# Four corners of the array for a chunk's value and output weight products: odd batches with the two heads exchanged

## Chip, cores and metric

One core of one Trainium2 chip. The metric is the device time of one execution in microseconds (us). Lower is better.

## What is computed

One pre-norm decoder layer on x of 4 x 512 rows and 256 columns: an attention across the rows of a group, a cross attention to a context of 4 batches of 64 rows, and a mixture of 8 experts. The change is in the cross attention (16 heads of 64, context `c`):

```python
q = (queries @ Wq + bq).reshape(bs, nq, H, D_KEY).transpose(0, 2, 1, 3)
k = (keys @ Wk + bk).reshape(bs, nk, H, D_KEY).transpose(0, 2, 1, 3)
v = (values @ Wv + bv).reshape(bs, nk, H, D_VALUE).transpose(0, 2, 1, 3)
att = jnp.einsum('bhqd,bhkd->bhqk', q, k) / np.sqrt(D_KEY).astype(np.float32)
att = jax.nn.softmax(att, axis=-1)
out = jnp.einsum('bhqk,bhkd->bhqd', att, v)
out = out.transpose(0, 2, 1, 3).reshape(bs, nq, H * D_VALUE)
return out @ Wo + bo
```

## The kernel before

The program is written engine by engine, each with its own instruction stream and with semaphores between them; the order of the work is the order in which the functions call their steps. There are four parts. Part 1 is the row attention and, between its steps, the preparation of the cross attention. Part 2 is the cross attention in 16 steps, one for each tile of 128 rows. Parts 3 and 4 are the routing and the experts.

The cross attention is folded into two tables that depend on the batch only. `G` is the query weight times the keys (line 765, `G_product`), so that the scores are the normalised rows times `G`. `H` is the values times the output weight (line 878, `pe_H`), so that the result is the transposed probabilities times `H`. Both are kept as two parts, `_hi` (rounded, copied by ScalarE: line 496 for G, line 889 for H) and `_lo` (the remainder, by VectorE: line 580 and line 897), and each later product is three matmuls (lines 917 to 919).

The 16 heads are handled in 8 chunks of two. For a chunk `c`, `V_T[:, c, b]` holds the values of batch `b`, head `2c` in partitions 0 to 63 and head `2c + 1` in 64 to 127; `Wo[:, c]` holds the matching rows of the output weight. Head 0's product of a batch is a 64x64 block of weights in the first 64 rows and first 64 columns of the array and gives partitions 0 to 63 of a bank, head 1's is in the other rows and columns and gives partitions 64 to 127. Two of the 4 batches stand side by side in one PSUM bank, and a chunk fills two banks, m = 0 and m = 1:

```python
for m in range(2):
    ps = bank_free(f"H{c}{m}")
    for b in (2 * m, 2 * m + 1):
        for rows in (slice(0, DK), slice(DK, P)):
            mm = t.matmul(ps[rows, (b % 2) * D:(b % 2 + 1) * D], V_T[rows, c, b], Wo[rows, c], ...)
    filled(mm, f"H{c}{m}")
```

`bank_free` makes TensorE wait until the bank's last user has been read, `filled` tells the readers. The banks of a chunk come from a table: `H_BANKS = ((4, 7), (5, 0), (1, 4), (7, 5), (4, 5), (7, 4), (5, 7), (4, 5))`. A bank is free when `H_lo` of its last user is made, as that is the second of its two readers.

The 8 chunks run in front of the first four steps of part 2 (`run_steps`, two chunks a step), mixed with the lead-in of the pipeline. TensorE's order is: chunks 0 and 1; transposes of the normalised rows of tile 0 (line 945); chunks 2 and 3; transposes of tile 1, scores of tile 0; chunks 4 and 5; transposes of tile 2, scores of tile 1; chunks 6 and 7; then the probability transposes of tile 0 (line 938), after which the 16 steps follow one another. After the scores, VectorE takes a maximum (`mx`, line 1160), subtracts it (`prob`, line 1165), and ScalarE takes the exponential (line 1026). On VectorE the chunks' `H_lo` stand in the same order as on TensorE, between `xT_lo` (line 1152), `mx`, `prob` and the sums of the exponentials (line 1138). On ScalarE chunk 5 stands behind the first exponential and the normalised rows of tile 2 (line 1200), chunk 7 behind the second and tile 3; `H_BEFORE_ACT` and `H_BEFORE_EXP` say so.

In part 1 the query weight is transposed into `WqT` (copied out of PSUM by VectorE, line 591; the bias's column by ScalarE, line 521). The scores' factor of `DK ** -0.5` is applied where G is copied. `of_head` gives the columns of G that belong to a head.

Of the kernel before, what the change touches and what calls it, by code (L numbers as in the profile page):

```python
# [13 lines left out]
def build_program(nc, A, out):  # L14
# [8 lines left out]
    ACT = mybir.ActivationFunctionType  # L23
    AX = mybir.AxisListType

    P = 128
    T, B, D = A["x"].shape
# [3 lines left out]
    MC = D // P  # L31
    HS = A["L0_attn_q_weight"].shape[1]
    HD = D // HS
    CB, CK, _ = A["ctx_1024"].shape
    HX = 16
    DK = A["L0_xattn_Wq"].shape[1] // HX
    HK = HX * CK
    NC = HX * DK // P
# [81 lines left out]
    with ctx:  # L120
# [6 lines left out]
        def overlay(*sets):  # L127
# [83 lines left out]
        bank = lambda i: ctx.enter_context(nc.psum_tensor(f"bank{i}", [P, 512], F32))  # L211
# [20 lines left out]
        WqT_ready, bq_placed, kv_ready = (  # L232
            sem(n) for n in ("WqT_ready", "bq_placed", "kv_ready"))
        G_hi_ready, G_ready = (sem(n) for n in ("G_hi_ready", "G_ready"))
        V_ready = sem("V_ready")
        H_hi_ready, H_ready = sem("H_hi_ready"), sem("H_ready")
# [52 lines left out]
        def bank_free(what):  # L289

            b, _, before = where[what]
            if before:
                nc.tensor.wait_ge(*before)
            return banks[b]

        def bank_full(eng, what):

            b, n, _ = where[what]
            eng.wait_ge(full[b], n + 1)
            return banks[b]  # L300

        def filled(mm, what):
            mm.then_inc(full[where[what][0]], 1)

        block = ctx.enter_context(nc.Block())
        v3 = lambda ap, a: ap.rearrange("p (a n) -> p a n", a=a)
        raw = lambda ap: ap.bitcast(F32)
        by_chunk = lambda bank: v3(bank[:], MC * CB)

        def of_head(G, c, h):  # L310

            return G[:].rearrange("p m b n -> p (m b) n")[:, :, c * P + h * DK:c * P + (h + 1) * DK]

# [114 lines left out]
        def act_part1(act):  # L430
            a = nc.scalar
# [60 lines left out]
            def G_evac(c):  # L492

                for h in range(2):
                    ps = bank_full(act, f"G{c}{h}")
                    a.activation(of_head(G_hi, c, h), by_chunk(ps), ACT.Copy, scale=DK ** -0.5).then_inc(G_hi_ready, 1)

            act.wait_ge(ident_ready, 1)
            a.activation(warm[:], ident[:, 0:1], ACT.Exp)
# [10 lines left out]
            ps = bank_full(act, "ctxT")  # L510
# [5 lines left out]
            ps = bank_full(act, "owT")  # L516
# [1 line left out]
            squares(0)  # L518
            xnT_evac(1)
            ps = bank_full(act, "cols")  # L520
            a.activation(WqT[:, :, D - 1], ps[:, 0:NC], ACT.Copy).then_inc(bq_placed, 1)
            a.activation(bias_cols[:], ps[:, 0:3 * NC], ACT.Copy).then_inc(cols_ready, 1)
            a.activation(b1_cols[:], ps[:, 32:32 + E * FC], ACT.Copy).then_inc(cols_ready, 1)

# [5 lines left out]
            ps = bank_full(act, "N")  # L530
# [6 lines left out]
            xnT_evac(3)  # L537
            q_evac(2)
            G_evac(0)
            mixT_evac(0)  # L540
            squares(2)
            KV_evac(1)
            G_evac(1)
            weights_of(2)
            q_evac(3)
            mixT_evac(1)
            squares(3)
            KV_evac(2)
            G_evac(2)
            weights_of(3)  # L550
            KV_evac(3)
# [12 lines left out]
        def dve_part1(dve, order):  # L564
            v = nc.vector
# [9 lines left out]
            def low_parts(c):  # L575

                for h in range(2):
                    ps = bank_full(dve, f"G{c}{h}")
                    dve.wait_ge(G_hi_ready, 2 * c + h + 1)
                    v.scalar_tensor_tensor(out=of_head(G_lo, c, h), in0=by_chunk(ps), scalar=DK ** -0.5,  # L580
                                           in1=raw(of_head(G_hi, c, h)), op0=ALU.mult,
                                           op1=ALU.subtract).then_inc(G_ready, 1)

            def WqT_evac(k):

                ps = v3(bank_full(dve, f"WqT{k}")[:], 2)
                for c in range(2):  # L590
                    ins = v.tensor_scalar(WqT[:, 2 * k + c, 0:D - 1], ps[:, c, 0:D - 1], ps[:, c, D - 1:D], None,
                                          ALU.subtract)
                ins.then_inc(WqT_ready, 1)

            def add_residual(j):
# [56 lines left out]
            for j in range(1, NJ):  # L652
# [4 lines left out]
            ps = bank_full(dve, "MT")  # L657
            v.tensor_tensor(MTs[:], v3(ps[:, 0:MC * P], MC), mask16[:].unsqueeze(1).to_broadcast([P, MC, P]),
                            ALU.mult).then_inc(MT_ready, 1)
            distances(0)  # L660
            WqT_evac(0)
            weigh(0)
            differences(1)
            WqT_evac(1)
            WqT_evac(2)
            distances(1)
            scale(0)
            WqT_evac(3)
            weigh(1)
            differences(2)  # L670
            low_parts(0)
            distances(2)
            scale(1)
            add_residual(0)
            weigh(2)
            differences(3)
            low_parts(1)
            distances(3)
            scale(2)
            add_residual(1)  # L680
            weigh(3)
            low_parts(2)
            statistics2(0)
            dve.wait_ge(consts_ready, 1)
# [181 lines left out]
        def pe_H(pe):  # L866

            t = nc.tensor

            def H_chunk(c):  # L870
                if c == 0:
                    pe.wait_ge(xn3_stored, 16)
                pe.wait_ge(V_ready, c + 1)
                for m in range(2):
                    ps = bank_free(f"H{c}{m}")
                    for b in (2 * m, 2 * m + 1):
                        for rows in (slice(0, DK), slice(DK, P)):
                            mm = t.matmul(ps[rows, (b % 2) * D:(b % 2 + 1) * D], V_T[rows, c, b], Wo[rows, c],
                                          start=True, stop=True)
                    filled(mm, f"H{c}{m}")  # L880
            return H_chunk

        def act_H(act):
            a = nc.scalar

            def H_chunk(c):
                for m in range(2):
                    ps = bank_full(act, f"H{c}{m}")
                    a.activation(H_hi[:, 2 * m:2 * m + 2, c], v3(ps[:], 2), ACT.Copy).then_inc(H_hi_ready, 1)
            return H_chunk  # L890

        def dve_H(dve):
            def H_chunk(c):
                for m in range(2):
                    ps = bank_full(dve, f"H{c}{m}")
                    dve.wait_ge(H_hi_ready, 2 * c + m + 1)
                    nc.vector.tensor_tensor(H_lo[:, 2 * m:2 * m + 2, c], v3(ps[:], 2), raw(H_hi[:, 2 * m:2 * m + 2, c]),
                                            ALU.subtract).then_inc(H_ready, 1)
            return H_chunk

# [779 lines left out]
        @block.scalar  # L1680
        def _(act):
            act_part1(act)
            act_part2(act)
            act_part3(act)
            act_part4(act)
# [32 lines left out]
```

## Time and profile before

| | |
|---|---|
| runs | 373.85, 373.59, 373.82 us (median 373.82) |
| span of the profiled execution | 370.1 us |
| instructions in it | 6439 |
| TensorE matmul busy | 319.9 us (86%) |
| VectorE busy | 287.2 us (78%) |
| ScalarE busy | 184.1 us (50%) |
| GpSimd busy | 195.2 us (53%) |

The span runs from the first to the last instruction of one profiled execution; the runs' times have in them what lies before and after it as well. Which of the three runs is nearest to the profiled one isn't told. Matmuls are pipelined, so that a busy TensorE is not one at its peak, and one fp32 matmul of the program shows as two records. All times of the rows below are in us from the start of the span. PE is TensorE (PEld its weight loads), DVE VectorE, ACT ScalarE, POOL GpSimd.

### The profile page before, as it was taken

What the parts mean: (1) busy time and instruction counts of PE and PEld (TensorE: products, weight loads), DVE (VectorE), ACT (ScalarE), POOL (GpSimd) and SP (SyncE); (2) the same over time, 40 slices, a digit from 0 to 9 for tenths busy, and PEclk for the clock granted to TensorE, in tenths of its full rate; (3) what the DMA queues carried; (4) which work ended last, traced back from release to release, by engine and by line L of the source; (5) the groups of instructions that cost most, each with busy time, mean ns of one, the idle gap of its engine ahead of it and who ended that gap; (6) DMA issues with size and microseconds to landing.
All of it is one profiled execution on the core that took longest, in us unless ns stands there. A gap on an engine that the chain in (4) does not pass through costs nothing.

```text
span 370.1 us, 6439 instructions
## 1 busy us (share of the span) xinstructions
PE 319.9 (86%) x2346; PEld 288.5 (78%) x2346; DVE 287.2 (78%) x659; ACT 184.1 (50%) x357; POOL 195.2 (53%) x247
## 2 busy tenths in 40 slices
PE   8889998899979999999999861116999999999991
PEld 7767886675569999999999851005999999999991
DVE  3898887948888988888888727787588699799850
ACT  2677554555545556775675432362317456652230
POOL 3787889713223468778878766003405515533222
PEclk9999999999999999999999985555999999999998
DMA  7950000000000306306215237001149657612222
GB/s 248 392 192 1 2 0 2 0 0 3 0 2 14 129 29 186 128 16 200 74 70 184 66 121 270 0 1 28 58 127 267 168 193 217 171 16 43 30 30 28
DMA packets 24047, 34.29 MB, mean 93 GB/s; under 512 B 1784, under 2 KB 20560, under 8 KB 23888
## 3 DMA queue, kind: packets, MB, share of 16 engines
q1 hardware_dynamic: 20112, 29.36, 23.7%
q0 software_dynamic: 3072, 4.20, 6.3%
q10 hardware_dynamic: 832, 0.32, 0.4%
q8 instruction: 19, 0.31, 0.3%
q14 instruction: 12, 0.10, 0.1%
HBM read 27.58 MB, written 6.29 MB: 92 GB/s over the span
## 4 chain that ended last, share of the span: by engine, by line
PE 69%; DVE 15%; POOL 7%; ACT 4%; issue 3%; DMA 1%; ACTq 0%; DVEq 0%; POOLq 0%
PE bank L917 12%; PE bank L919 12%; PE bank L918 12%; PE q_banks L917 4%; PE q_banks L918 4%; PE q_banks L919 4%; PE bank L938 4%; DVE flags_all L1271 3%; PE q_banks L718 2%; PE bank L1444 2%; PE bank L736 2%; PE bank L752 2%; PE bank L982 1%; POOL acc L410 1%; DMA X<-in_x 1%
## 5 line engine op out<-in xcount | busy, mean ns | idle before, releaser
L1569 POOL DMA_INDIRECT out_x<-ybuf,idx x16 | 26.3, 1641 | 59.8 <-DVE ybuf L1588 57.7
L1046 POOL TENSOR_TENSOR prob<-prob,rsum 128x1024 f32<-128x1024 f32 x16 | 30.5, 1905 | 18.8 <-DVE rsum L1144 17.3
L917 PE MATMUL bank<-H_hi,PT_hi 128*128 128x256 f32 x128 | 36.3, 284 | 1.7 <-DVE PT_lo L1115 1.7
L917 PE MATMUL bank<-W_hi,h_hi 128*128 128x256 f32 x128 | 37.2, 291 | 0.0
L919 PE MATMUL bank<-H_hi,PT_lo 128*128 128x256 f32 x128 | 36.2, 283 | 0.0
L918 PE MATMUL bank<-H_lo,PT_hi 128*128 128x256 f32 x128 | 36.2, 283 | 0.0
L919 PE MATMUL bank<-W_hi,h_lo 128*128 128x256 f32 x128 | 36.2, 283 | 0.0
L918 PE MATMUL bank<-W_lo,h_hi 128*128 128x256 f32 x128 | 36.2, 283 | 0.0
L1549 POOL DMA_INDIRECT xg<-xn_rows,idx x16 | 18.5, 1158 | 29.5 <-DVE idx L1615 25.3
L1026 ACT ACTIVATE prob<-prob 128x1024 f32<-128x1024 f32 x16 | 16.9, 1059 | 33.5 <-DVE prob L1165 33.4
L1526 ACT ACTIVATE hbuf<-bank,b_cols 128x256 f32<-128x256 f32 x32 | 13.4, 472 | 40.1 <-PE bank L919 40.1
L1099 POOL TENSOR_TENSOR W_lo<-W_raw,W_hi 128x1024 fp32r<-128x1024 f32 x12 | 28.6, 2386 | 0.0
L917 PEld LDWEIGHTS bank<-H_hi,PT_hi 128*128 128x128 f32 x128 | 24.5, 191 | 2.7 <-issue 2.1
L918 PEld LDWEIGHTS bank<-H_lo,PT_hi 128*128 128x128 f32 x128 | 24.5, 191 | 0.5
L917 PEld LDWEIGHTS bank<-W_hi,h_hi 128*128 128x128 f32 x128 | 24.7, 193 | 0.2 <-DVE h_lo L1649 0.2
L918 PEld LDWEIGHTS bank<-W_lo,h_hi 128*128 128x128 f32 x128 | 24.6, 192 | 0.0
L919 PEld LDWEIGHTS bank<-W_hi,h_lo 128*128 128x128 f32 x128 | 24.5, 192 | 0.0
L919 PEld LDWEIGHTS bank<-H_hi,PT_lo 128*128 128x128 f32 x128 | 24.5, 191 | 0.0
L1647 DVE CAST h_hi<-hbuf 128x512 fp32r<-128x512 f32 x32 | 13.8, 432 | 13.2 <-ACT hbuf L1526 13.1
L1649 DVE TENSOR_TENSOR h_lo<-hbuf,h_hi 128x512 fp32r<-128x512 f32 x32 | 22.2, 692 | 1.1
L1600 DVE TENSOR_TENSOR W_lo<-W_raw,W_hi 128x2048 fp32r<-128x2048 f32 x10 | 22.7, 2284 | 0.0
L1115 DVE TENSOR_TENSOR PT_lo<-bank,PT_hi 128x512 fp32r<-128x512 f32 x32 | 20.1, 669 | 0.6 <-ACT PT_hi L998 0.6
(269 smaller groups left out, 1063.6 us busy)
## 6 DMA issues: line engine op xcount, KB each, us to landing
W_raw<-in_L_ffn_W SPq DMA_DIRECT2D x16, 1024.0 KB, 5.7
X<-in_x SPq DMA_DIRECT2D x4, 512.0 KB, 6.2
xn_rows<-xn SPq DMA_DIRECT2D x16, 128.0 KB, 1.7
out_x<-X SPq DMA_DIRECT2D x4, 512.0 KB, 3.5
Wq<-in_L_xattn_Wq SPq DMA_DIRECT2D x1, 1024.0 KB, 10.9
Wk<-in_L_xattn_Wk SPq DMA_DIRECT2D x1, 1024.0 KB, 13.8
Wv<-in_L_xattn_Wv SPq DMA_DIRECT2D x1, 1024.0 KB, 15.0
Wo<-in_L_xattn_Wo SPq DMA_DIRECT2D x1, 1024.0 KB, 16.9
```

The costliest lines, as they stand in the source:

```text
L917: t.matmul(out_ps, hi, rhs_hi, start=first, stop=False)
L918: t.matmul(out_ps, hi, rhs_lo, start=False, stop=False)
L919: return t.matmul(out_ps, lo, rhs_hi, start=False, stop=last_one)
L938: mm = t.transpose(banks[4 + g][:, c * P:(c + 1) * P], flat[:, o:o + P], ident[:])
L1026: a.activation(prob[:, s], prob[:, s], ACT.Exp).then_inc(exp_ready, 1)
L1046: g.tensor_tensor(prob[:, s], prob[:, s], rsum[:, s].unsqueeze(2).to_broadcast([P, HX, CK]), ALU.mult).then_inc(prob_ready, 1)
L1099: nc.gpsimd.tensor_tensor(lo[at], W[at], raw(hi[at]), ALU.subtract).then_inc(ready, 1)
L1115: v.tensor_tensor(PT_lo[:, cur.slot, c], v3(banks[4 + g][:], 4), raw(PT_hi[:, cur.slot, c]), ALU.subtract).then_inc(PT_ready, 1)
L1549: g.indirect_dma_start(xg[:, s, h], None, xn3_dram, bass.IndirectOffsetOnAxis(ap=idx[:, e, h:h + 1], axis=0), bounds_check=last_row, oob_i ...
L1569: g.indirect_dma_start(out_flat, bass.IndirectOffsetOnAxis(ap=idx[:, e, h:h + 1], axis=0), ybuf[:, h], None, bounds_check=last_row, oob_is ...
L1600: v.tensor_tensor(lo[at], W[at], raw(hi[at]), ALU.subtract).then_inc(late, 1)
L1649: v.tensor_tensor(h_lo[:, fs], hbuf[:, g_ % 2], raw(h_hi[:, fs]), ALU.subtract).then_inc(h_ready, 1)
```

## The change

In an odd batch the two heads of a chunk change places in the output: head 0's product goes to partitions 64 to 127 of the bank, head 1's to 0 to 63. Batches 0 and 2 now share the chunk's first bank, 1 and 3 its second, so that the four products of an even and an odd batch use the four 64x64 corners of the array. Both banks are waited for ahead of the chunk's first product; the first is told full after batch 2, the second after batch 3. The copies of H write every other batch. So that the probabilities, whose order is that of G's columns, meet the same order in H, `of_head` exchanges the two heads' columns of G in the odd batches. That makes the pattern of its copies longer by one loop, and the factor `DK ** -0.5` moves from them into `WqT` and the bias's column; `G_lo` becomes a plain subtraction.

```diff
@@ -305,11 +305,14 @@
         block = ctx.enter_context(nc.Block())
         v3 = lambda ap, a: ap.rearrange("p (a n) -> p a n", a=a)
         raw = lambda ap: ap.bitcast(F32)
-        by_chunk = lambda bank: v3(bank[:], MC * CB)
+        by_chunk = lambda bank: bank[:].rearrange("p (a b n) -> p a b n", b=2, n=DK)
 
         def of_head(G, c, h):
 
-            return G[:].rearrange("p m b n -> p (m b) n")[:, :, c * P + h * DK:c * P + (h + 1) * DK]
+            first = G[:, 0, 0, c * P + h * DK:c * P + (h + 1) * DK]
+            across, along = first.ap
+            return bass.AP(first.tensor, first.offset,
+                           [across, [2 * HK, MC * CB // 2], [HK + (DK if h == 0 else -DK), 2], along])
 
 
 
@@ -493,7 +496,7 @@
 
                 for h in range(2):
                     ps = bank_full(act, f"G{c}{h}")
-                    a.activation(of_head(G_hi, c, h), by_chunk(ps), ACT.Copy, scale=DK ** -0.5).then_inc(G_hi_ready, 1)
+                    a.activation(of_head(G_hi, c, h), by_chunk(ps), ACT.Copy).then_inc(G_hi_ready, 1)
 
             act.wait_ge(ident_ready, 1)
             a.activation(warm[:], ident[:, 0:1], ACT.Exp)
@@ -518,7 +521,7 @@
             squares(0)
             xnT_evac(1)
             ps = bank_full(act, "cols")
-            a.activation(WqT[:, :, D - 1], ps[:, 0:NC], ACT.Copy).then_inc(bq_placed, 1)
+            a.activation(WqT[:, :, D - 1], ps[:, 0:NC], ACT.Copy, scale=DK ** -0.5).then_inc(bq_placed, 1)
             a.activation(bias_cols[:], ps[:, 0:3 * NC], ACT.Copy).then_inc(cols_ready, 1)
             a.activation(b1_cols[:], ps[:, 32:32 + E * FC], ACT.Copy).then_inc(cols_ready, 1)
 
@@ -577,9 +580,8 @@
                 for h in range(2):
                     ps = bank_full(dve, f"G{c}{h}")
                     dve.wait_ge(G_hi_ready, 2 * c + h + 1)
-                    v.scalar_tensor_tensor(out=of_head(G_lo, c, h), in0=by_chunk(ps), scalar=DK ** -0.5,
-                                           in1=raw(of_head(G_hi, c, h)), op0=ALU.mult,
-                                           op1=ALU.subtract).then_inc(G_ready, 1)
+                    v.tensor_tensor(of_head(G_lo, c, h), by_chunk(ps), raw(of_head(G_hi, c, h)),
+                                    ALU.subtract).then_inc(G_ready, 1)
 
             def WqT_evac(k):
 
@@ -588,8 +590,8 @@
 
                 ps = v3(bank_full(dve, f"WqT{k}")[:], 2)
                 for c in range(2):
-                    ins = v.tensor_scalar(WqT[:, 2 * k + c, 0:D - 1], ps[:, c, 0:D - 1], ps[:, c, D - 1:D], None,
-                                          ALU.subtract)
+                    ins = v.tensor_scalar(WqT[:, 2 * k + c, 0:D - 1], ps[:, c, 0:D - 1], ps[:, c, D - 1:D],
+                                          DK ** -0.5, ALU.subtract, ALU.mult)
                 ins.then_inc(WqT_ready, 1)
 
             def add_residual(j):
@@ -871,13 +873,14 @@
                 if c == 0:
                     pe.wait_ge(xn3_stored, 16)
                 pe.wait_ge(V_ready, c + 1)
-                for m in range(2):
-                    ps = bank_free(f"H{c}{m}")
-                    for b in (2 * m, 2 * m + 1):
-                        for rows in (slice(0, DK), slice(DK, P)):
-                            mm = t.matmul(ps[rows, (b % 2) * D:(b % 2 + 1) * D], V_T[rows, c, b], Wo[rows, c],
-                                          start=True, stop=True)
-                    filled(mm, f"H{c}{m}")
+                halves = (slice(0, DK), slice(DK, P))
+                ps = [bank_free(f"H{c}{m}") for m in range(2)]
+                for b in range(CB):
+                    for h in range(2):
+                        mm = t.matmul(ps[b % 2][halves[h ^ (b % 2)], (b // 2) * D:(b // 2 + 1) * D],
+                                      V_T[halves[h], c, b], Wo[halves[h], c], start=True, stop=True)
+                    if b >= 2:
+                        filled(mm, f"H{c}{b % 2}")
             return H_chunk
 
         def act_H(act):
@@ -886,7 +889,7 @@
             def H_chunk(c):
                 for m in range(2):
                     ps = bank_full(act, f"H{c}{m}")
-                    a.activation(H_hi[:, 2 * m:2 * m + 2, c], v3(ps[:], 2), ACT.Copy).then_inc(H_hi_ready, 1)
+                    a.activation(H_hi[:, m:CB:2, c], v3(ps[:], 2), ACT.Copy).then_inc(H_hi_ready, 1)
             return H_chunk
 
         def dve_H(dve):
@@ -894,7 +897,7 @@
                 for m in range(2):
                     ps = bank_full(dve, f"H{c}{m}")
                     dve.wait_ge(H_hi_ready, 2 * c + m + 1)
-                    nc.vector.tensor_tensor(H_lo[:, 2 * m:2 * m + 2, c], v3(ps[:], 2), raw(H_hi[:, 2 * m:2 * m + 2, c]),
+                    nc.vector.tensor_tensor(H_lo[:, m:CB:2, c], v3(ps[:], 2), raw(H_hi[:, m:CB:2, c]),
                                             ALU.subtract).then_inc(H_ready, 1)
             return H_chunk
 
```

The order of TensorE between the first and the second scores, with chunks 4 (banks 4 and 5) and 5 (banks 7 and 4); a row is a matmul of the program, `xk` that many of them, and the semaphores for which the first waits stand behind it. Before:

```order
L919 MATMUL bank1<-G_hi,xT_lo 128x512
L878 MATMUL bank4<-Wo,V_T 64x256 [waits H_ready,V_ready]
L878 MATMUL bank4<-Wo,V_T 64x256 x3
L878 MATMUL bank5<-Wo,V_T 64x256 [waits H_ready]
L878 MATMUL bank5<-Wo,V_T 64x256 x3
L878 MATMUL bank7<-Wo,V_T 64x256 [waits H_ready,V_ready]
L878 MATMUL bank7<-Wo,V_T 64x256 x3
L878 MATMUL bank4<-Wo,V_T 64x256 [waits H_ready]
L878 MATMUL bank4<-Wo,V_T 64x256 x3
L945 MATMUL bank6<-ident,xn2 128x128 [waits xT_ready,xn2_ready]
```

Of the change:

```order
L922 MATMUL bank1<-G_hi,xT_lo 128x512
L880 MATMUL bank4<-Wo,V_T 64x256 [waits H_ready,V_ready]
L880 MATMUL bank4<-Wo,V_T 64x256
L880 MATMUL bank5<-Wo,V_T 64x256 x2
L880 MATMUL bank4<-Wo,V_T 64x256 x2
L880 MATMUL bank5<-Wo,V_T 64x256 x2
L880 MATMUL bank7<-Wo,V_T 64x256 [waits H_ready,V_ready]
L880 MATMUL bank7<-Wo,V_T 64x256
L880 MATMUL bank4<-Wo,V_T 64x256 x2
L880 MATMUL bank7<-Wo,V_T 64x256 x2
L880 MATMUL bank4<-Wo,V_T 64x256 x2
L948 MATMUL bank6<-ident,xn2 128x128 [waits xT_ready,xn2_ready]
```

A chunk's two banks now take turns, and its second wait has gone to its front: the first product of chunk 5, in bank 7, stands behind the wait for bank 4, which chunk 4's `H_lo` frees.

The order of TensorE ahead of the first scores, with chunks 2 (banks 1 and 4) and 3 (banks 7 and 5). Before:

```order
L878 MATMUL bank1<-Wo,V_T 64x256 [waits x1_ready,V_ready]
L878 MATMUL bank1<-Wo,V_T 64x256 x3
L878 MATMUL bank4<-Wo,V_T 64x256 [waits H_ready]
L878 MATMUL bank4<-Wo,V_T 64x256 x3
L878 MATMUL bank7<-Wo,V_T 64x256 [waits H_ready,V_ready]
L878 MATMUL bank7<-Wo,V_T 64x256 x3
L878 MATMUL bank5<-Wo,V_T 64x256 [waits H_ready]
L878 MATMUL bank5<-Wo,V_T 64x256 x3
L945 MATMUL bank6<-ident,xn2 128x128 [waits xT_ready,xn2_ready]
L945 MATMUL bank6<-ident,xn2 128x128
L917 MATMUL bank0<-G_hi,xT_hi 128x512 [waits H_ready,xT_ready]
```

Of the change:

```order
L880 MATMUL bank1<-Wo,V_T 64x256 [waits H_ready,x1_ready,V_ready]
L880 MATMUL bank1<-Wo,V_T 64x256
L880 MATMUL bank4<-Wo,V_T 64x256 x2
L880 MATMUL bank1<-Wo,V_T 64x256 x2
L880 MATMUL bank4<-Wo,V_T 64x256 x2
L880 MATMUL bank7<-Wo,V_T 64x256 [waits H_ready,V_ready]
L880 MATMUL bank7<-Wo,V_T 64x256
L880 MATMUL bank5<-Wo,V_T 64x256 x2
L880 MATMUL bank7<-Wo,V_T 64x256 x2
L880 MATMUL bank5<-Wo,V_T 64x256 x2
L948 MATMUL bank6<-ident,xn2 128x128 [waits xT_ready,xn2_ready]
```

The matmuls are as many as before; chunk 3 waits for bank 5 ahead of its products in bank 7.

## Rows read from the trace of the kernel before

**Rows 1.** The page: its first line, and the engines' shares of the chain.

```profile
span 370.1 us, 6439 instructions
PE 69%; DVE 15%; POOL 7%; ACT 4%; issue 3%; DMA 1%; ACTq 0%; DVEq 0%; POOLq 0%
```

**Rows 2.** The chain that ended last, by time: start us, us, what (xrecords).

```profile
30.05 3.72 PE q_banks L718 x16
...
58.37 1.06 PE q_banks L765 x8
...
85.12 3.60 PE bank L878 x32
...
89.33 0.23 PE bank L918
...
91.89 1.29 DVE mx L1160 x2
...
95.95 0.49 ACT H_hi L889
...
104.07 0.70 DVE H_lo L897
```

**Rows 3.** TensorE in order of time, 78 to 107 us: start us, us, what [idle before].

```profile
85.05 3.67 PE L878 MATMUL bank<-Wo,V_T 64*64 64x256 f32 x32
88.65 0.44 PE L945 MATMUL bank<-ident,xn 128*128 128x128 f32 x2
88.85 0.48 PE L917 MATMUL bank<-G_hi,xT_hi 128*128 128x512 f32 x1
...
91.78 2.81 PE L878 MATMUL bank<-Wo,V_T 64*64 64x256 f32 x24
95.02 1.08 PE L878 MATMUL bank<-Wo,V_T 64*64 64x256 f32 x8 [0.44 <-DVE H_lo L897]
96.03 0.44 PE L945 MATMUL bank<-ident,xn 128*128 128x128 f32 x2
...
104.91 1.16 PE L938 MATMUL bank<-ident,prob 128*128 128x128 f32 x8 [1.27 <-DVE H_lo L897]
```

**Rows 4.** VectorE in order of time, 78 to 107 us.

```profile
84.32 2.47 DVE L897 TENSOR_TENSOR H_lo<-bank,H_hi 128x512 fp32r<-128x512 f32 x4
86.70 0.42 DVE L1152 TENSOR_TENSOR xT_lo<-bank,xT_hi 128x256 fp32r<-128x256 f32 x1
87.04 1.40 DVE L897 TENSOR_TENSOR H_lo<-bank,H_hi 128x512 fp32r<-128x512 f32 x2
...
94.29 1.28 DVE L897 TENSOR_TENSOR H_lo<-bank,H_hi 128x512 fp32r<-128x512 f32 x2
96.53 1.29 DVE L897 TENSOR_TENSOR H_lo<-bank,H_hi 128x512 fp32r<-128x512 f32 x2 [0.97 <-ACT H_hi L889]
```

**Rows 5.** ScalarE in order of time, 78 to 107 us.

```profile
92.91 0.60 ACT L889 ACTIVATE H_hi<-bank 128x512 fp32r<-128x512 f32 x1 [3.26 <-PE bank L878]
...
95.86 1.06 ACT L889 ACTIVATE H_hi<-bank 128x512 fp32r<-128x512 f32 x2
```

**Rows 6.** Groups of instructions, whole span: xcount | busy us, mean ns | idle before.

```profile
L897 DVE TENSOR_TENSOR H_lo<-bank,H_hi 128x512 fp32r<-128x512 f32 x16 | 10.4, 685 | 2.3 <-ACT H_hi L889 2.3
L889 ACT ACTIVATE H_hi<-bank 128x512 fp32r<-128x512 f32 x16 | 9.2, 596 | 8.0 <-PE bank L878 8.0
L580 DVE SCALAR_TENSOR_TENSOR G_lo<-bank,G_hi 128x512 fp32r<-128x512 f32 x10 | 6.4, 680 | 2.8 <-ACT G_hi L496 2.8
L496 ACT ACTIVATE G_hi<-bank 128x512 fp32r<-128x512 f32 x10 | 5.5, 602 | 8.6 <-PE bank L765 8.6
```

**Rows 7.** Lines 591 and 650: duration ns min/median/max, first and last start us.

```profile
L591 DVE TENSOR_SCALAR WqT<-bank x8: 476/478/482, 20.9 to 32.0; 128x255 f32<-128x255 f32 x8
L650 DVE TENSOR_SCALAR xn<-X,mv,rstd x3: 414/502/557, 8.0 to 8.8; 128x256 f32<-128x256 f32 x3
```

**Rows 8.** Line 878's records from 95.02 to 95.3 us, the first of chunk 5's second half.

```profile
L878 PE MATMUL bank<-Wo,V_T x4: 376/402/427, 95.0 to 95.3; 64*64 64x256 f32 x4
```

## The prediction

> **What bounds the kernel now.** I read the page first [rows 1]: the span is 370.1 us and the chain that ended last runs 69% over TensorE and 15% over VectorE. The median of the runs is 373.82 us, so about 3.7 us lie around the span; the sum below is made against the span and carried over to the median as it is. A change of under 0.2% (0.75 us) is what a measurement of this kernel can hardly tell from none.
>
> Then I looked at what the edit touches: the products of chunks 0 to 7 (line 878), between 80 and 105 us. Two things stand in the chain of waits there [rows 2]. Before the first scores the chain runs through 32 records of line 878, that is TensorE bounds. After the scores it leaves TensorE: VectorE (`mx` and more), ScalarE (up to `H_hi`), VectorE (`H_lo`), and it comes back to TensorE only with the probability transposes of line 938. So the same products lie on the path once, and beside it twice. From 104.9 us on the chain is TensorE, step after step, and whatever is won or lost by then is carried to the end.
>
> One matmul of line 878 shows as two records. How much of the array is in use is read from the chain [rows 2]: the full 128x128 products of line 718 go one after the other, 16 records in 3.72 us, 0.23 us a record; line 878 does 32 records in 3.60 us, so two run at a time (heads 0 and 1, each in its corner). Four at a time would halve that.
>
> **What it removes, step one: chunks 2 and 3.** Today both take 3.67 us from 85.05 us, two transposes follow at 88.65, and the first scores start at 88.85 [rows 3]. A half chunk of 8 records takes 1.08 us to its last result (the row at 95.02) and lets the next start after 3.60/4 = 0.90 us; at four at a time these are the figures of a whole chunk. Chunk 2 still starts at 85.05. Chunk 3 now waits for both its banks at once: the later one is freed by the third of the four `H_lo` that start at 84.32 and take 2.47 us, 0.60 us apart and 0.68 us long, so at 86.2 [rows 4]. It runs from 86.25 to about 87.2, the transposes to 87.45. Then the scores meet their next wait, the one for chunk 2's first `H_lo`: it starts at 87.04 behind `xT_lo` (86.70) on VectorE [rows 4] and would not start earlier, since VectorE works without a pause from 84.3 to there; its `H_hi` is ready by then (85.05 + 1.08 + 0.60 = 86.7). It ends at 87.72, so the scores start at 87.8 in place of 88.85: **1.05 us won**. What is late next is VectorE. `mx`, which follows the scores, starts 1.05 us earlier too, at 90.8 for 91.89 [rows 2], as the copies of chunk 3 that stand ahead of it come forward with their products.
>
> **What it adds, step two: chunks 5 and 7.** Today the first half of chunk 5 runs right after chunk 4 (the 24 records at 91.78), and only its second half, in bank 4, waits for chunk 4's `H_lo` [rows 3]. Both bank waits now stand ahead of the chunk's first product, so the whole of it waits. This `H_lo` starts at 94.29 and ends at 94.97 [rows 4], and TensorE goes on at 95.02. At four at a time the chunk ends when its second half ends today, 1.08 us later at 96.10, and the transposes at 96.03 and the next scores are not moved. But its first bank is then full only at 96.10, where today it has long been full: ScalarE copies 0.05 us behind a full bank (91.78 + 1.08 = 92.86 against 92.91 [rows 5]), so at 96.15 where today it comes at 95.86, after `prob` and `xn` [rows 5]. That is 0.3 us, and nothing hides it: VectorE waits for exactly this copy, 0.97 us today [rows 4], and after its two `H_lo` it goes straight on to sums, `xT_lo` and the next `mx`. **0.3 us lost.** Chunk 7 is the same pattern 7.5 us later (`H_lo` at 104.07 in [rows 2]); its `H_lo` is what the transposes of line 938 wait for, 1.27 us today [rows 3]. **Another 0.3 us lost.**
>
> **The small edits.** The copies of G keep their count and size. `G_lo` goes from a scalar_tensor_tensor of 680 ns to a tensor_tensor, which at 128x512 from the same kind of memory takes 685 ns (`H_lo`); ScalarE's copy with a scale takes 602 ns, without one 596 (`H_hi`) [rows 6]. The swapped column order is a third loop in the pattern over the same 512 elements; the contiguous `H_lo` and the strided `G_lo` rows agree within 5 ns, so I cost it at nothing. The scale moves into `WqT`, whose tensor_scalar gets a second operation: 478 ns today, and the nearest row with two operations, line 650, runs 414 to 557 ns [rows 6, 7]. Two of the eight lie on the chain, so this is -0.13 to +0.16 us; I take zero, since the medians of 478 and 502 ns are nearest to no difference. The copy of the query bias into `WqT` (128x8) changes only its scale.
>
> **The sum**: -1.05 + 0.3 + 0.3 = -0.45 us, a span of 369.65 and **373.4 us** against the median.
>
> The unknown in it is one price: two blocks that share a row half but not a column half. No row shows that pair. Two rows stand near it. Line 765 has blocks that share all columns but no rows, and does 8 records in 1.06 us, also two at a time [rows 2]; and the scores' products take in 512 columns [rows 3] every 0.23 us (line 918 in [rows 2]), so the stream into one row half carries twice what one record of line 878 asks for (256 columns in 0.23 us). Both speak for four at a time, which I take. Ends: four at a time without any loss, -0.45 us; in between, the second block of a row half comes one record behind the first and shows its weight load, which I read as the 0.05 us by which a first record (427 ns) is longer than the others (376 ns) [rows 8]. The first bank is then full 0.1 us later and the second some 0.35; ScalarE's second copy is 0.48 us behind its first anyway, so a chunk loses 0.1 us more and the sum is -0.25 us.
> The Trainium skill, TensorE: Matmul & The Clock Gate (Part 3: Packing small matmuls), reports 16 blocks of 32x32 at 10.6 times the speed; no run here shows it, and by it the sum would be the -0.45 us.
>
> **The rivals.**
> *Two at a time, as now (slower).* If blocks of one row half exclude each other, a chunk takes 8 steps as today, and the first step is worth nothing: chunks 2 and 3 end at 88.65 again. The second step then costs the whole half that can no longer run ahead: chunk 5 starts at 95.02, its first bank is full two steps of 0.225 us before the end, 1.08 + 0.90 - 0.45 = 1.53 us later, and ScalarE copies at 96.60 in place of 95.86: 0.74 us lost, and as much again at chunk 7. Together +1.5 us, **375.3 us**; with a weight load of 0.05 us shown at each of three changes of block, some 0.2 us more, 375.5. It decides as soon as a chunk alone takes more than about 1.6 us. For it speaks that no row shows such a pair; against it the two rows above. It is also the case in which the change does not do what it says.
> The Trainium skill has two rules that would give this case. TensorE: Matmul & The Clock Gate (Part 3) says a weight load overlaps a running matmul only if the row group differs. TensorEngine Tiling (Restrictions and Gotchas) says that different row tiles cannot use one PSUM bank at once. The trace disagrees with the second as far as it can be seen: heads 0 and 1 write one bank from two row halves, and do so two at a time [rows 2].
> *The losses do not show (faster).* If a first bank were full 0.79 us after the chunk's start (95.86 - 0.05 - 95.02), ScalarE would find it ready, and the whole 1.05 us stays: **372.8 us**. Against it: each block has four records in a row, and half a chunk with the same four takes 1.08 us today [rows 3].
> *Part of both.* Two streams into a row half slow each other to a chunk of about 1.4 us: the first step still wins nearly all of its 1.05 us, the chunks lose some 0.5 us each, and the time is about that of before.
>
> **How the numbers follow.** Four at a time, with or without the one record's lag, 0.63: 373.4 us, its own range 373.1 to 373.7. Partly, 0.07: 373.8. Two at a time, 0.20: 375.3. Faster than the sum, 0.10: 372.8 or below. The range takes in the rival that is slower and leaves out half of the faster one: 372.8 to 375.4. Faster by over 0.2% takes the last case and a little of the first, 0.13; slower the second rival and a little of the part case, 0.23; the rest, 0.64, is within 0.2%.
>
> **What would show it.** Right: the records of the product line stand in 16s of about 1.1 us; the first scores start about 1 us earlier, at 87.8; the pause of VectorE ahead of the `H_lo` of chunks 5 and 7 grows from 0.97 to about 1.3 us; and line 938 starts about 0.45 us earlier than 104.91. Wrong: a chunk that takes 1.8 us or more alone, or first scores that start at 88.8 still; or a `WqT`, `G_hi` or `G_lo` whose mean moves by more than 50 ns.

## The result and the profile after

The changed kernel takes 378.38 us (median of 4 runs, 376.88 to 379.17) against 373.70 (4 runs, 373.37 to 373.85) before: ratio 1.0137, 95% interval 1.0109 to 1.0165. In a second set, with the experiments below, it took 377.46 us (6 runs) against 373.63 (29 runs), ratio 1.0107 (1.0067 to 1.0148). The forecast was 373.4 us, from 372.8 to 375.4: the change is slower, and by more than the range allowed.

Where the time went in the two profiled executions, by four marks in TensorE's order:

| stretch | before, us | after, us | difference |
|---|---|---|---|
| start to chunk 0's first product | 80.27 | 82.69 | +2.42 |
| from there to the first probability transposes | 24.64 | 25.47 | +0.83 |
| from there to the second (one step) | 6.82 | 9.24 | +2.42 |
| from there to the end | 258.4 | 259.9 | +1.5 |

The four differences add up to 7.2 us, more than the 4.7 of the medians, since the two profiled executions are not alike: every execution here takes 1.7 to 1.9 us more than its span, so the one before, with its span of 370.1 us, took about 372, while the changed one is the longest of its four (379.17). The marks before that are not shown above:

```profile
80.27 3.67 PE L878 MATMUL bank<-Wo,V_T 64*64 64x256 f32 x32
84.71 0.41 PE L945 MATMUL bank<-ident,xn 128*128 128x128 f32 x2 [0.77 <-DVE G_lo L580]
...
111.73 1.03 PE L938 MATMUL bank<-ident,prob 128*128 128x128 f32 x8
```

TensorE of the changed kernel in order of time (start us, us, what [idle before]; line 878 is now 880, 945 is 948, 938 is 941):

```profile
82.69 1.96 PE L880 MATMUL bank<-Wo,V_T 64*64 64x256 f32 x32
87.12 0.41 PE L948 MATMUL bank<-ident,xn 128*128 128x128 f32 x2 [2.48 <-DVE G_lo L583]
87.55 2.29 PE L880 MATMUL bank<-Wo,V_T 64*64 64x256 f32 x32
89.77 0.44 PE L948 MATMUL bank<-ident,xn 128*128 128x128 f32 x2
90.28 0.47 PE L920 MATMUL bank<-G_hi,xT_hi 128*128 128x512 f32 x1
...
93.21 1.09 PE L880 MATMUL bank<-Wo,V_T 64*64 64x256 f32 x16
96.54 1.98 PE L880 MATMUL bank<-Wo,V_T 64*64 64x256 f32 x16 [2.24 <-DVE H_lo L900]
98.46 0.69 PE L948 MATMUL bank<-ident,xn 128*128 128x128 f32 x2
...
102.17 1.09 PE L880 MATMUL bank<-Wo,V_T 64*64 64x256 f32 x16
105.51 1.09 PE L880 MATMUL bank<-Wo,V_T 64*64 64x256 f32 x16 [2.24 <-DVE H_lo L900]
108.16 1.94 PE L941 MATMUL bank<-ident,prob 128*128 128x128 f32 x8 [1.56 <-DVE H_lo L900]
...
117.40 1.03 PE L941 MATMUL bank<-ident,prob 128*128 128x128 f32 x8
```

A chunk, 16 records, takes 1.09 us where half a chunk took 1.08 [rows 3]: four blocks do run at a time. From chunk 0's first product to the first scores it is 7.59 us (82.69 to 90.28) where it was 8.58, so 0.99 us are won. But chunk 5 takes 1.98 us, and the transposes of line 941 1.94 in place of 1.16: nearly twice, and they are the same instructions. VectorE's wait ahead of the two `H_lo` of chunk 5, 0.97 us before [rows 4], and of chunk 7, 0.97 us before as well, shows the same difference between the two chunks, of which only chunk 5 was slow:

```profile
99.25 1.29 DVE L900 TENSOR_TENSOR H_lo<-bank,H_hi 128x512 fp32r<-128x512 f32 x2 [2.25 <-ACT H_hi L892]
...
107.33 1.29 DVE L900 TENSOR_TENSOR H_lo<-bank,H_hi 128x512 fp32r<-128x512 f32 x2 [1.36 <-ACT H_hi L892]
```

The reason is in the table by stretches of the same execution (us; busy us of PE, PEld, DVE, ACT and POOL with their instructions; PEclk, the granted share of TensorE's clock; DMA share, GB/s):

```profile
87.10:96.50 9.40, 6.99 (x64) 4.29 (x64) 8.34 (x16) 5.16 (x11) 1.87 (x4) 0.99 0.01 3
96.50:99.85 3.35, 3.31 (x21) 2.08 (x22) 1.10 (x2) 2.18 (x5) 0.00 (x0) 0.51 0.00 0
99.90:106.60 6.70, 4.46 (x43) 2.70 (x41) 5.97 (x11) 2.64 (x5) 2.58 (x2) 1.00 0.00 0
106.80:113.50 6.70, 5.34 (x18) 4.69 (x19) 4.27 (x7) 2.87 (x6) 2.60 (x2) 0.51 0.01 2
113.60:117.40 3.80, 3.80 (x30) 3.62 (x28) 2.48 (x4) 0.16 (x1) 0.00 (x0) 1.00 0.00 0
```

Twice the granted clock falls to half, that is from 2.4 to 1.2 GHz. Stretches of a quarter of a microsecond place the falls at 96.4 us (PEclk 0.73 from 96.25 to 96.5) and at 106.6 us (0.71 from 106.5 to 106.75). The first is the end of the pause of 2.24 us at chunk 5. The second is not right behind the pause of 2.24 us at chunk 7: chunk 7 still takes its 1.09 us at full clock, and the clock falls as the next pause begins, the 1.56 us ahead of the probability transposes. In all three pauses TensorE waits for an `H_lo`. Before, the same stretches ran at full clock:

```profile
95.00:104.90 9.90, 8.02 (x54) 4.91 (x55) 7.93 (x14) 5.90 (x11) 2.59 (x2) 1.00 0.00 0
104.90:111.70 6.80, 6.79 (x46) 6.20 (x47) 5.79 (x10) 2.02 (x5) 2.61 (x2) 1.00 0.01 2
```

So the theory became: **the products are as fast as forecast, but the shorter they are the longer TensorE pauses, and the pauses let its clock fall; the work behind them runs at half speed.** The Trainium skill, TensorE: Matmul & The Clock Gate (Part 1), describes half rate as the state TensorE is in when it has done little, and full rate as earned by activity; these rows agree (0.51 behind the pauses, 0.99 and 1.00 ahead of them).

The first and the last line of the table by marks do not need the change. The profile of the kernel before with filled pauses (below), which has nothing of the change, shows both: chunk 0 starts at 82.79 us, with the clock at 0.50 from 21.5 to 24.8, and the last stretch is 259.9 us. The last stretch goes with the routing, through which the clock is at half in all 13 profiles: for 37.5 us in three of them (last stretch 257.5 to 257.8 us), 41.0 in three, the kernel before among them (258.4 to 259.0), and 44.4 in seven, the changed kernel among them (259.9 to 260.0). Whether the change makes the long form likelier is not shown. Such differences come and go from execution to execution: 35 executions of the kernel before took 371.70 to 376.06 us, with a mean granted clock of 0.944 in the shortest and 0.930 in the longest. The 3 runs shown ahead of the prediction lay closer together by chance.

### The profile page after: what moved, and what is told of

It reads as the page before. It is cut to its first block, busy times and chain, and to the rows that moved or that the text cites. A ratio compares the mean times of both kernels' runs of the same rounds, so it can differ in the third digit from the quotient of the medians.

```text
span 377.3 us, 6440 instructions
## 1 busy us (share of the span) xinstructions
PE 322.0 (85%) x2346; PEld 291.5 (77%) x2346; DVE 287.0 (76%) x659; ACT 183.8 (49%) x357; POOL 195.1 (52%) x247
## 4 chain that ended last, share of the span: by engine, by line
PE 74%; DVE 12%; POOL 6%; ACT 4%; issue 2%; DVEq 0%; POOLq 0%; ACTq 0%
PE bank L920 13%; PE bank L922 12%; PE bank L921 12%; PE q_banks L920 4%; PE q_banks L921 4%; PE q_banks L922 4%; PE bank L941 4%; PE q_banks L720 3%; DVE flags_all L1274 3%; PE bank L775 2%; PE bank L1447 2%; PE bank L738 2%; PE bank L754 1%; PE bank L985 1%; PE bank L880 1%
```

## The experiments

Each was timed beside the kernel before, in 6 to 12 executions; "before" was 373.61 to 373.93 us in every set. The ratios lie within 0.001 of those of the mean times, and so are not quite those of the medians (for the filled kernel 0.9965 by the means and 0.9947 by the medians).

**Filling the pauses.** Unread matmuls of the identity with itself go into a bank that is free already, in the four places where TensorE waits:

```diff
+            def keep_busy(n, bank):
+                for _ in range(n):
+                    t.matmul(bank[:, 0:P], ident[:], ident[:], start=True, stop=True)
...
-                ps = [bank_free(f"H{c}{m}") for m in range(2)]
+                ps = [bank_free(f"H{c}0")]
+                if c in FILL:
+                    keep_busy(FILL[c], ps[0])
+                ps.append(bank_free(f"H{c}1"))
...
+                if c == 1:
+                    keep_busy(FILL_LEAD, bank_free("H20"))
+                if c == NC - 1:
+                    pe.wait_ge(H_ready, H_last[7])
+                    keep_busy(FILL_END, banks[7])
```

> The changed kernel with matmuls that nobody reads (identity times identity, into a bank that is already free) in TensorE's pauses: 9 ahead of the first transposes, 9 each ahead of the second bank wait of chunks 5 and 7, 5 ahead of the probability transposes. Clock theory (the pauses of 2.24 us that the shorter products leave are where the granted clock falls to half): the granted clock stays 1.0 from 80 to 120 us, the way from the first product of chunk 0 to the first probability transposes takes 24.2 us (24.64 before, 25.47 changed) and the next step 6.98 us as before (9.40 changed); the whole is 373.3 us, or up to 376 where the clock also falls in part 1. Rival, the four corners or the new waits themselves slow what follows: the next step stays near 9.4 us and the whole near 378.

Measured: 371.64 us, ratio 0.9971 (0.9949 to 0.9993). TensorE of this kernel (its line 888 is the products, 875 the unread ones, 954 the probability transposes):

```profile
80.26 1.96 PE L888 MATMUL bank<-Wo,V_T 64*64 64x256 f32 x32
82.14 2.27 PE L875 MATMUL bank<-ident 128*128 128x128 f32 x18
...
91.76 2.27 PE L875 MATMUL bank<-ident 128*128 128x128 f32 x18
93.98 1.09 PE L888 MATMUL bank<-Wo,V_T 64*64 64x256 f32 x16
...
104.49 1.16 PE L954 MATMUL bank<-ident,prob 128*128 128x128 f32 x8 [0.26 <-DVE H_lo L913]
...
111.37 1.04 PE L954 MATMUL bank<-ident,prob 128*128 128x128 f32 x8
```

From chunk 0 to the transposes 24.23 us, 0.41 less than before (forecast: 0.45 less), and the step after it 6.88 us. (The 6.98 and 9.40 us of the expectation were read from the chain, whose second mark lies 0.16 us later; between these rows it was 6.82 before and 9.24 changed.) The clock is at 1.00 from 80 to 118 us. The whole is 1.7 us below the 373.3 expected; the kernel before, filled (below), has a lower median too. Adding work that nobody reads takes about 6 us off the changed kernel (377.46 and 378.38 against 371.64). The rival falls.

**The small edits alone**: scale in `WqT`, `G_lo` as a subtraction.

```diff
-                    a.activation(of_head(G_hi, c, h), by_chunk(ps), ACT.Copy, scale=DK ** -0.5).then_inc(G_hi_ready, 1)
+                    a.activation(of_head(G_hi, c, h), by_chunk(ps), ACT.Copy).then_inc(G_hi_ready, 1)
...
-                    ins = v.tensor_scalar(WqT[:, 2 * k + c, 0:D - 1], ps[:, c, 0:D - 1], ps[:, c, D - 1:D], None,
-                                          ALU.subtract)
+                    ins = v.tensor_scalar(WqT[:, 2 * k + c, 0:D - 1], ps[:, c, 0:D - 1], ps[:, c, D - 1:D],
+                                          DK ** -0.5, ALU.subtract, ALU.mult)
...
```

> The kernel before with the small edits alone: the factor in WqT and the bias's column, G_lo as a plain subtraction; column order and products of H as before. Clock theory: nothing on the path changes, 373.7 us. Rival, the small edits cost the 2.4 us that the changed kernel was late by before chunk 0's first product: 376.1 us, and the products of chunk 0 start at 82.7 in place of 80.27.

Measured: 373.76 us, ratio 1.0010 (0.9986 to 1.0034), the products of chunk 0 at 80.42 us. They cost nothing. In this profiled execution the clock fell at the probability transposes (0.50 from 105.1 to 108.4 us), behind a pause of 1.27 us that the kernel before has too [rows 3]: the fall there can come without the change.

**Chunks 5 and 7 as before, the rest at four corners.**

```diff
+        OLD = (5, 7)
+        batches = lambda c, m: slice(2 * m, 2 * m + 2) if c in OLD else slice(m, CB, 2)
...
+                if c in OLD:
+                    for m in range(2):
+                        ps = bank_free(f"H{c}{m}")
+                        for b in (2 * m, 2 * m + 1):
+                            for rows in halves:
+                                mm = t.matmul(ps[rows, (b % 2) * D:(b % 2 + 1) * D], V_T[rows, c, b], Wo[rows, c],
+                                              start=True, stop=True)
+                        filled(mm, f"H{c}{m}")
+                    return
...
```

> The changed kernel with chunks 5 and 7 in the old arrangement (each bank's half behind its own wait, heads not exchanged), the others at four corners. Clock theory: TensorE's pauses there shrink to those of before (some 0.5 us), the granted clock stays 1.0, and the 1.05 us of chunks 2 and 3 stay won: 372.7 us. Rival, any shortening of the products lets the clock fall: 376 us or more.

Measured: 372.34 us, ratio 0.9973 (0.9944 to 1.0002), so not clear of no change. From chunk 0 to the probability transposes it takes 23.65 us (80.53 to 104.18), 0.99 us less than before: without the moved waits the whole first step stays won.

```profile
80.53 1.96 PE L893 MATMUL bank<-Wo,V_T 64*64 64x256 f32 x32
...
94.30 1.08 PE L886 MATMUL bank<-Wo,V_T 64*64 64x256 f32 x8 [1.30 <-DVE H_lo L913]
...
101.83 1.08 PE L886 MATMUL bank<-Wo,V_T 64*64 64x256 f32 x8 [1.44 <-DVE H_lo L913]
104.18 1.62 PE L954 MATMUL bank<-ident,prob 128*128 128x128 f32 x8 [1.27 <-DVE H_lo L913]
```

TensorE's pauses ahead of the second halves are 1.30 and 1.44 us, not the 0.5 expected, as the work ahead of them is shorter. The clock stayed at 1.00 up to there and fell at the transposes (0.50 from 104.8 to 108.0 us), so the clock part of the expectation held at chunks 5 and 7 only.

**Both waits first, two at a time.**

```diff
+                both = [bank_free(f"H{c}{m}") for m in range(2)]
                 for m in range(2):
-                    ps = bank_free(f"H{c}{m}")
+                    ps = both[m]
```

> The kernel before with both bank waits ahead of each chunk's first product, products in the old order and two at a time. The prediction's arithmetic without the clock: chunks 5 and 7 lose 0.74 us each, 375.2 us. Clock theory in its strong form (a pause of about 1.6 us alone is enough): the granted clock falls to half after chunk 5 or 7 and the time is 377 us or more. Rival, the waits cost nothing: 373.7 us.

Measured: 374.28 us, ratio 1.0031 (1.0010 to 1.0052).

```profile
92.09 1.94 PE L879 MATMUL bank<-Wo,V_T 64*64 64x256 f32 x16
95.43 1.94 PE L879 MATMUL bank<-Wo,V_T 64*64 64x256 f32 x16 [1.39 <-DVE H_lo L898]
...
106.42 1.43 PE L939 MATMUL bank<-ident,prob 128*128 128x128 f32 x8 [0.71 <-DVE H_lo L898]
```

From chunk 0 (80.52) to the transposes it takes 25.90 us, 1.26 more than before; the arithmetic of the rival said 1.48. The strong form is not borne out: the pauses came to 1.39 us, not 1.6, and behind them, between chunks of 1.94 us, the clock stayed at 1.00, from 80 to 113 us. In the whole kernel the median rises by 0.66 us only, half of that loss. All 12 executions have a mean granted clock of 0.939 or more, where the kernel before has 0.930 to 0.944; that the shorter pause at the transposes (0.71 us for 1.27) does this is likely, but not shown.

**The changed kernel again**, unchanged, in the set of the next three.

> The changed kernel once more, beside the next three, in many more executions. Clock theory: the pauses at chunks 5 and 7 let the clock fall in most executions, so the median stays above that of before, at 375 to 378.5 us, and the executions scatter by several us with their mean granted clock. Rival, the four executions timed first were unlucky in the clock of other stretches (part 1 and the routing), and the change itself costs nothing: 373.2 us.

Measured: 377.46 us, 375.72 to 378.92, ratio 1.0107. The executions go with their mean granted clock: 375.72 at 0.926, 376.69 and 377.14 at 0.921 and 0.922, 377.78 to 378.92 at 0.917, where the kernel before has 0.930 to 0.944. In this profile the clock falls three times between 80 and 114 us, the first time behind the pause ahead of the first transposes:

```profile
86.00:89.30 3.30, 3.30 (x32) 1.95 (x32) 2.57 (x6) 2.02 (x5) 1.52 (x3) 0.50 0.00 0
...
96.30:99.50 3.20, 3.20 (x22) 2.05 (x15) 1.12 (x3) 1.87 (x5) 0.00 (x0) 0.50 0.00 0
...
106.50:113.20 6.70, 5.51 (x18) 4.84 (x19) 4.27 (x7) 2.70 (x6) 2.60 (x2) 0.50 0.01 2
```

From chunk 0 (81.10 us) to the probability transposes (107.69) it takes 26.59 us, 1.95 more than before, and the step behind them 9.38, 2.56 more.

**Two pauses filled.** `FILL_LEAD` and `FILL_END` are 0, so only the 9 matmuls at chunk 5 and at chunk 7 stay.

> The changed kernel with unread matmuls in two pauses only, 9 each ahead of the second bank wait of chunks 5 and 7. Clock theory, with these two pauses as its place: nearly all is back, 371.6 to 372.5 us. Rival, the pause of 2.48 us ahead of the first transposes or that ahead of the probability transposes is the one that counts: it stays near the changed kernel, 375 us or more.

Measured: 373.65 us, ratio 1.0004 (0.9980 to 1.0027). These two pauses are worth 3.8 us against the 377.46 of the same set, but not everything: another 2.0 us, to the 371.64 of the first set, is in the other two. The result lies between the two ends of the expectation.

**Three pauses filled**: those two and the one ahead of the probability transposes (`FILL_END` 5, `FILL_LEAD` 0).

> The changed kernel with unread matmuls ahead of the second bank wait of chunks 5 and 7 (9 each) and ahead of the probability transposes (5), none in the pause of 2.48 us ahead of the first transposes. If the pause at the probability transposes was what was still missing: 371.6 us, as with all four pauses filled. If it was the first pause: 373.6 us, as with chunks 5 and 7 alone.

Measured: 373.32 us, ratio 0.9997 (0.9977 to 1.0017). By the edits, then, what was missing is mostly the pause of 2.5 us ahead of the first transposes, where the second profile of the changed kernel shows its fall at 86 us. The profile of this run (of 373.39 us) doesn't show it: behind a pause of 2.62 us there its clock stays at 1.00 from 80 to 112 us. So this share is read from medians of two sets alone.

**The kernel before, filled**: 3, 2, 2 and 5 unread matmuls in its smaller pauses at the same places (`keep_busy` as above).

> The kernel before with unread matmuls in its smaller pauses at the same four places (3, 2, 2 and 5 of them). If the gain of the filled changed kernel came from the four corners: 373.6 us, as before. If the kernel before too loses to a falling clock at the probability transposes in part of its executions, as in the profile of the small edits alone (a fall of 3.4 us at 105 us): 372.2 us, and the four corners are then worth only the rest, some 0.5 us.

Measured: 371.95 us, ratio 0.9983 (0.9954 to 1.0012): half of its executions are at 371.92 or below, but four are at 373.5 to 375.9, so the interval does not exclude no change. It leaves for the four corners, as the change has them, the 0.3 us between this and the 371.64 of the filled changed kernel, two medians of different sets.

**The arrangement of chunks 5 and 7 as before, and all pauses filled**: the kernel of the third experiment with 9, 5, 5 and 5 unread matmuls.

> Chunks 5 and 7 in the old arrangement, the others at four corners, and unread matmuls in all four pauses (9 ahead of the first transposes, 5 each ahead of the second half of chunks 5 and 7, 5 ahead of the probability transposes). If the two gains add up: 0.6 us under the changed kernel with such matmuls, 371.0 us, with the way from chunk 0 to the first probability transposes at 23.65 us and no fall of the clock from 80 to 120 us. Rival, the matmuls delay the second halves: no better than 371.6 us.

Measured: 370.70 us, ratio 0.9944 (0.9917 to 0.9972). Chunk 0 to the transposes takes 23.63 us, with the clock at 1.00 throughout:

```profile
80.50 1.96 PE L904 MATMUL bank<-Wo,V_T 64*64 64x256 f32 x32
...
104.13 1.16 PE L967 MATMUL bank<-ident,prob 128*128 128x128 f32 x8
```

**It beats both kernels**, the one before by 2.9 us and the filled one before, in the same set, by 1.25 (medians; 8 of its 12 executions are shorter than any of that one).

**The same with part 1's pause filled.** Six more unread matmuls ahead of the second query product.

```diff
             def q_product(j):
+                if j == 1:
+                    for _ in range(FILL_Q1):
+                        t.matmul(bank_free("q10")[:, 0:P], ident[:], ident[:], start=True, stop=True)
```

> The version with chunks 5 and 7 in the old arrangement and all four pauses filled, and 6 unread matmuls in part 1 as well, ahead of the wait for the transposed rows of the second query product (the pause of 1.4 us at 19 us after which the changed kernel's clock fell at 21 us). If its slower executions (372.6 us and more, mean granted clock 0.935) are those in which the clock falls there: they are gone, and all executions lie from 369.9 to 371 us, median 370.3. Rival, they come from the clock's release after the routing: a third of the executions stays above 372.5 us, median 370.7.

Measured: 370.76 us (6 executions), ratio 0.9915 (0.9884 to 0.9945) against a before of 373.93. Five lie from 370.13 to 371.08 and one at 372.52, where 4 of 12 were above 372.5 without. That is the direction expected, but too few to tell, and the median is no better. The profile is of the long one and speaks for the rival: its clock is at 1.00 from the start up to the routing, and there at half for 41.0 us, where the profile without this filling (of 370.58 us) has 37.5; chunk 0 starts 0.8 us later as well, with no fall ahead of it.

**Half the products, no corners.** To part the pauses from the corners: the kernel of "both waits first", with the odd batches' products left out; the tables then hold the even batches' values twice.

```diff
-                    for b in (2 * m, 2 * m + 1):
+                    for b in (2 * m,):
...
-                    a.activation(H_hi[:, 2 * m:2 * m + 2, c], v3(ps[:], 2), ACT.Copy).then_inc(H_hi_ready, 1)
+                    a.activation(H_hi[:, 2 * m:2 * m + 2, c], twice(ps), ACT.Copy).then_inc(H_hi_ready, 1)
...
```

> The kernel before with both bank waits ahead of each chunk, and with the odd batches' products left out (the readers copy the even batch's half of a bank twice, so the tables hold wrong values for odd batches): a chunk is 4 products, two at a time, as short as one at four corners, and TensorE's pauses become those of the changed kernel (2.2 us at chunks 5 and 7, 2.5 us ahead of the first transposes), with none of its four corners. Clock theory, pauses alone: the clock falls as in the changed kernel, in the profile at chunk 5 or 7 and at the probability transposes, and the median is 376 to 378.5 us. Rival, it is the four corners that let the clock fall: the granted clock stays 1.0 from 80 to 115 us, 373.2 us as forecast for the changed kernel.

Measured: 378.20 us (6 executions), ratio 1.0120 (1.0082 to 1.0157), the same as the changed kernel.

```profile
93.36 1.08 PE L880 MATMUL bank<-Wo,V_T 64*64 64x256 f32 x8
96.70 1.97 PE L880 MATMUL bank<-Wo,V_T 64*64 64x256 f32 x8 [2.26 <-DVE H_lo L899]
...
105.75 1.08 PE L880 MATMUL bank<-Wo,V_T 64*64 64x256 f32 x8 [2.26 <-DVE H_lo L899]
108.01 1.94 PE L940 MATMUL bank<-ident,prob 128*128 128x128 f32 x8 [1.18 <-DVE H_lo L899]
```

```profile
96.00:99.50 3.50, 2.80 (x11) 1.67 (x12) 1.94 (x4) 2.90 (x5) 0.00 (x0) 0.59 0.00 0
...
106.50:113.00 6.50, 5.32 (x21) 4.45 (x18) 4.27 (x7) 3.01 (x7) 2.60 (x2) 0.53 0.00 0
```

The falls are at the same two places as in the first profile of the changed kernel, at the end of chunk 5's pause and in the one behind chunk 7, although every product runs two at a time and half of them are gone. A kernel that leaves out half of these products is thereby 4.6 us slower than the one that does them all. It is the pauses, not the corners.

## Why the prediction was wrong

Point by point, by its own steps:

- *Four at a time*, the price that was unknown: right, without any loss. A chunk takes 1.09 us; forecast 1.08.
- *Step one*, 1.05 us won at the first scores: right in size, 0.99 us (and 0.99 for the whole way where chunks 5 and 7 kept their order).
- *Step two*, 0.3 us lost at each of chunks 5 and 7: right where the clock holds. VectorE's wait at chunk 7 is 1.36 us for the 1.3 forecast, and the sum of the three terms, -0.45 us, measures -0.41 in the filled kernel.
- *The small edits* at nothing: right. `WqT` has a median of 477 ns for 478, `G_lo` a mean of 678 for 680, `G_hi` 603 for 602.
- *What failed* is the sentence of step two that the transposes "and the next scores are not moved". It took TensorE's own longer pauses (0.44 to 2.24 us at chunk 5 [rows 3]) as free, because the chain goes past them, and priced everything behind them at full clock. The same holds for the first step, whose won time is partly a pause of 2.48 us where there were 0.77. In the profiled execution chunk 5 and the start of the scores behind it, and later the probability transposes and most of the scores behind them, ran at half clock: +0.83 and +2.42 us where -0.45 and 0 stood, 3.7 us together. In the second profile, where the clock also fell ahead of the first scores, it is +1.95 and +2.56, 5.0 us together. No rival had it: the slower one had another cause, blocks that exclude each other, and its 375.3 us still was too low.
- *The base.* The 3 runs before lay within 0.26 us, and the prediction took that for the kernel's scatter. Over 35 executions it is 4.4 us, most of it with the granted clock. That alone would have asked for a wider range. The 3.7 us between the profiled span and the median were not all around the span either: that part is 1.7 to 1.9 us in every execution, and the rest is that the profile was of one of the shorter executions. The forecast is a difference, so this moved only its base.

What stays open: why an execution falls at one pause and not at another (at 86.0 us in the second profile of the changed kernel, not in the first; right behind the pause at chunk 5, but not behind the equal one at chunk 7), and so which share of the median each pause has; the runs give it only in sum.

## What to carry to other kernels

Making TensorE's work shorter where it then waits for another engine does not only win nothing there: the wait can cost the clock of the work behind it, so read the granted clock and the pauses together before a pause is priced at zero. A few unread matmuls in such a pause can hold the clock and cost nothing, if a free bank is at hand and they end before the wait does. Take a gain where TensorE is what the others wait for (here the chunks ahead of the first scores), and leave alone the ones that wait themselves.

## What the runs showed of the hardware

- Four 64x64 blocks in four corners, each pair of a row half and a column half used at once, run four at a time in fp32: 16 records in 1.09 us, against 8 in 1.08 for two corners.
- Two row halves that share column halves wrote two banks at once, each bank from both row halves, without loss of time. The Trainium skill, TensorEngine Tiling (Restrictions and Gotchas), would not have two row tiles in one bank at once; the trace disagrees for tiles in different partitions.
- In the two profiles of the changed kernel and the one with half the products, the clock fell to half within 0.5 us of the end of a pause of 2.24 to 2.48 us, or in the shorter pause (1.56 and 1.18 us) behind chunk 7. A pause of this length was not always followed by a fall: behind that ahead of chunk 7 (2.24 to 2.26 us) the chunk ran at full clock in all three, and that ahead of the first transposes, unfilled and 2.48 to 2.62 us long in six profiles, was followed by a fall in one.
- Pauses of 1.39 us between chunks of 1.94 us were not followed by a fall in the profile; one of 1.27 us at the probability transposes was in two profiles and not in that of the kernel before, and one of 1.57 us there, in the kernel with the pauses at chunks 5 and 7 filled, was not.
